# A gated cross-attention and feed-forward block on one core: a load order, a rotary pair and a centring step rewritten

## The chip, the core and the metric

The kernel runs on one NeuronCore of one Trainium2 chip. The core has five engines that run side by side and talk through semaphores: TensorE (PE in the profile: matrix products into PSUM; its weight loads are listed as PEld), VectorE (DVE), ScalarE (ACT), GpSimd (POOL, which reads and writes SBUF only) and SyncE (SP, which here only starts transfers). Each takes its instructions strictly in the order in which the program lists them. The metric is device time in microseconds (us) for the whole program, lower is better.

## What is computed

Four sequences of 1024 tokens with width 256 attend to 154 memory tokens of their own through 4 query heads that share one key and value head, with rotary positions; then comes a feed-forward layer whose weights are rounded to -1, 0 or 1. Both branches are gated by a tanh and added to the residual.

```python
x = x + tanh(g_xattn[0]) * xattn(layernorm(x), ctx_1024, mask)
x = x + tanh(g_ffn[0])   * ffn(layernorm(x))

def xattn(x, mem_seq, mem_mask):
    xn, mn = rmsnorm(x, rms_scale), rmsnorm(mem_seq, rms_scale)   # normed * (1 + scale)
    q = einsum('BTD,NDH->BTNH', xn, q_w)             # 4 heads of 64
    k, v = einsum('BSD,cKDH->cBSKH', mn, kv_w)       # 1 head of 64
    q, k = rope(q, S + arange(T)) * 64 ** -0.5, rope(k, arange(S))
    # rope: [x1 * cos - x2 * sin, x2 * cos + x1 * sin] on the halves of a head
    probs = softmax(where(mem_mask, q @ k, MASK_FILL))
    return einsum('BTNH,NHD->BTD', probs @ v, out_w)

def ffn(x):
    h = gelu(x @ ternary(W1).T + b1)                 # exact gelu, 1024 wide
    return h @ ternary(W2).T + b2
```

## The kernel before, in words

The 4096 tokens are 8 groups (`NG`) of 512 tokens, and a group is 4 tiles (`NT`) of 128 tokens. A group passes three stages: its attention in step i, the first layer of its feed-forward in step i+1 and the second layer in step i+2, so a step of the main loop (`step`) works on three groups at once. Steps 0 and 1 (`FIRST`, `SECOND`), together with what prepares weights, keys and values (`BEFORE`), are the function `fill` of each engine, whose calls are in an order written by hand. Each engine has its own `fill` and its own `step`; nothing else sets the order. Steps 2 to 9 run through `loop`, and their order of calls is the same on either side of the change.

Float32 accuracy is had by splitting an operand into a rounded part and a remainder (`_hi` and `_lo`): ACT copies the rounded part out of PSUM, DVE subtracts it from PSUM and so makes the remainder, and PE multiplies hi by hi, hi by lo and lo by hi. The remainders of the combined value and output weights (`vw_rest`) are made on DVE; the tuple `VW_ON_POOL` that could send some to POOL is empty.

The pieces that the change touches:

- **Queries.** `q(s, t)` and `q_first(s)` project a tile into a PSUM bank `ps_m` (256 columns: head, half, element). `rotate` (L976 to L994) reads the bank twice on DVE: once times the row's norm and the cosines into `q_cos` (L989), once times the norm and the sines into `q_sin` (L992). POOL adds the two with the halves swapped (`add_rotated`, L463), PE transposes the sum (`q_T`, L1447), ACT and DVE split it (`q_hi`, `q_lo`), and PE multiplies it by the keys (`scores`).
- **Centring.** The layer norm's mean is taken out of the query weights instead of the tokens. ACT scales `wq` rows by 1 + `rms_scale` (`scale_wq`, twice 128x256), PE sums them over all 256 inputs with a matrix of ones (`sum_wq`), DVE subtracts the sum divided by 256 (`centre_wq`, L872, twice 128x256), and ACT and DVE split the result into `wq_hi` and `wq_lo`.
- **Loads.** SP starts, in this order: the memory tokens and their four tails, group 0 of x (`x_sb[0]`), the key tables, the query tables, `wo`, `w1t`, `w2t`, group 1 of x (`x_sb[1]`, L349) and `b1`. ACT starts the identity, the scale row, the two gates, `wk`, `wv` and `wq`.
- **Statistics of group 1.** `sums1(FIRST)` (L952, four BN_STATS on DVE) needs group 1 of x.
- **Weights' means.** ACT adds up the absolute values of both weight matrices (`sum_weights`, L638) as soon as each is there; thresholds and ternary weights come from these.

## Time and profile before

| | us |
|---|---|
| median of three runs | 308.63 |
| lowest and highest run | 308.58 and 308.81 |
| the profiled execution: its own time | 309.19 |
| the profiled execution: span of the core | 307.4 |
| PE busy in the span | 295.4 |
| DVE busy | 243.2 |
| ACT busy | 234.3 |
| POOL busy | 131.1 |

The profile records one execution. Its own time is 1.79 us above the span (what lies before the first and after the last instruction) and 0.56 us above the median of the runs. The page gives, for each engine, how long it was busy, and the same in 40 slices with the clock that TensorE was granted. It has a chain of waits followed back from the last instruction, groups of instructions by line, and the transfers. The trace behind it can be asked for the instructions of one engine in order of time, for what an engine waited for, and for busy time by stretches. Matrix products are pipelined, so one listed with 0.28 us may be followed by the next after 0.12 us: what a row of many costs is read from start to start.

### The profile page before, as it was taken

The numbers are of one execution on the slowest core, as the hardware profiler recorded it, in microseconds if no ns is written. First come the engines' busy times: TensorE is split into PE (matmuls) and PEld (weight loads), VectorE is DVE, ScalarE is ACT, GpSimd is POOL, SyncE is SP. The second block draws the span as 40 slices with busy tenths as digits, with TensorE's granted clock in tenths as the row PEclk, the third lists the DMA queues.
The fourth block names the chain that finished last, engine by engine and source line by source line (L and its number), as shares of the span: only waits on it lengthen the run. The fifth ranks groups of instructions, "written<-read, shape, count | busy, mean of one in ns | idle before, by whom it ended". The sixth has DMA issues, their size and how long they took to land.

```text
span 307.4 us, 6780 instructions
## 1 busy us (share of the span) xinstructions
PE 295.4 (96%) x2119; PEld 274.6 (89%) x2119; DVE 243.2 (79%) x819; ACT 234.3 (76%) x601; POOL 131.1 (43%) x152
## 2 busy tenths in 40 slices
PE   5996999989999999999999999999999999999996
PEld 5975999878999899989998899989998999889886
DVE  2589899999987889779886899878977897567443
ACT  2596787898697967897588959796788958883581
POOL 8376878692246305522334414630542333511300
PEclk9999899999999999999999999999999999999999
DMA  6970000200202002100201010100210000100202
GB/s 204 286 243 2 0 3 0 71 0 2 69 3 68 2 0 70 53 17 2 68 13 55 0 54 15 51 17 0 71 52 17 2 0 11 61 3 0 70 0 68
DMA packets 12281, 13.27 MB, mean 43 GB/s; under 512 B 823, under 2 KB 11696, under 8 KB 12256
## 3 DMA queue, kind: packets, MB, share of 16 engines
q1 hardware_dynamic: 11452, 12.29, 12.6%
q10 hardware_dynamic: 708, 0.46, 0.5%
q0 software_dynamic: 96, 0.21, 0.4%
q8 instruction: 13, 0.21, 0.3%
q14 instruction: 12, 0.10, 0.1%
HBM read 8.76 MB, written 4.19 MB: 42 GB/s over the span
## 4 chain that ended last, share of the span: by engine, by line
PE 85%; DVE 7%; issue 2%; ACT 2%; DMA 1%; POOL 0%; ACTq 0%; DVEq 0%
PE ps_m L1293 22%; PE ps_h L1293 22%; PE ps_m L1526 17%; PE ps_s L1293 9%; PE ps_t L1301 4%; PE ps_t L1471 4%; PE ps_t L1447 2%; DMA gate_row<-in_gates 1%; PE ps_t L1546 1%; PE ps_m L1546 1%; DVE s_neg L1025 1%; PE ps_t L1479 1%; DVE pT_lo L938 1%; ACT hT_hi L699 1%; ACT h_all L699 1%
## 5 line engine op out<-in xcount | busy, mean ns | idle before, releaser
L487 POOL TENSOR_TENSOR prob<-prob,p_inv 128x512 f32<-128x512 f32 x32 | 34.2, 1069 | 66.8 <-DVE p_inv L1041 66.7
L1086 DVE TENSOR_TENSOR hT_lo<-h_all,hT_hi 128x512 fp32r<-128x512 f32 x64 | 42.2, 686 | 18.6 <-ACT hT_hi L699 18.6
L1293 PE MATMUL ps_h<-x1nT_hi,w_tern 128*128 128x512 f32 x128 | 54.4, 425 | 1.2 <-ACT hT_hi L699 0.9
L1526 PE MATMUL ps_m<-w_tern,hT_hi 128*128 128x256 f32 x224 | 55.2, 287 | 0.0
L1526 PE MATMUL ps_m<-w_tern,hT_lo 128*128 128x256 f32 x224 | 53.6, 279 | 0.0
L665 ACT ACTIVATE prob<-s_neg,s_min 128x154 f32<-128x154 f32 x128 | 52.4, 416 | 1.2 <-DVE s_min L1036 1.1
L699 ACT ACTIVATE h_all<-ps_h,b_sb 128x512 f32<-128x512 f32 x64 | 44.6, 697 | 8.2 <-PE ps_h L1293 7.0
L1293 PE MATMUL ps_h<-x1nT_lo,w_tern 128*128 128x512 f32 x128 | 50.6, 395 | 0.0
L463 POOL TENSOR_TENSOR q_cos<-q_cos,q_sin 128x256 f32<-128x256 f32 x32 | 23.6, 738 | 58.4 <-DVE q_sin L992 57.6
L1293 PE MATMUL ps_m<-vw_hi,pT_hi 128*128 128x256 f32 (+1 forms) x160 | 45.5, 284 | 0.0
L1293 PE MATMUL ps_m<-vw_hi,pT_lo 128*128 128x256 f32 (+1 forms) x160 | 44.8, 280 | 0.0
L1293 PE MATMUL ps_m<-vw_lo,pT_hi 128*128 128x256 f32 (+1 forms) x160 | 44.7, 279 | 0.0
L699 ACT ACTIVATE hT_hi<-ps_h,b_sb 128x512 fp32r<-128x512 f32 x64 | 44.7, 698 | 0.0
L1526 PEld LDWEIGHTS ps_m<-w_tern,hT_lo 128*128 128x128 f32 x224 | 42.2, 188 | 0.0
L1526 PEld LDWEIGHTS ps_m<-w_tern,hT_hi 128*128 128x128 f32 x224 | 42.1, 188 | 0.0
L938 DVE TENSOR_TENSOR pT_lo<-ps_t,pT_hi 128x512 fp32r<-128x512 f32 (+1 forms) x64 | 30.2, 482 | 10.8 <-ACT pT_hi L642 10.7
L642 ACT ACTIVATE pT_hi<-ps_t 128x512 fp32r<-128x512 f32 (+1 forms) x64 | 27.3, 444 | 9.0 <-PE ps_t L1471 8.8
L1293 PEld LDWEIGHTS ps_m<-vw_hi,pT_hi 128*128 128x128 f32 x160 | 30.0, 188 | 1.2
L1293 PEld LDWEIGHTS ps_h<-x1nT_hi,w_tern 128*128 128x128 f32 x128 | 24.1, 188 | 7.4 <-ACT hT_hi L699 3.8
L1293 PEld LDWEIGHTS ps_m<-vw_lo,pT_hi 128*128 128x128 f32 x160 | 30.1, 188 | 0.6
L1293 PEld LDWEIGHTS ps_m<-vw_hi,pT_lo 128*128 128x128 f32 x160 | 30.0, 187 | 0.0
L642 ACT ACTIVATE qT_hi<-ps_t 128x256 fp32r<-128x256 f32 x32 | 12.1, 377 | 23.2 <-PE ps_t L1447 23.2
(162 smaller groups left out, 778.2 us busy)
## 6 DMA issues: line engine op xcount, KB each, us to landing
x_sb<-in_x SPq DMA_DIRECT2D x8, 512.0 KB, 3.5
out_x<-x_both SPq DMA_DIRECT2D x8, 384.0 KB, 2.5
h_all<-in_w1t SPq DMA_DIRECT2D x1, 1024.0 KB, 11.1
w_raw<-in_w2t SPq DMA_DIRECT2D x1, 1024.0 KB, 13.4
out_x<-x_both SPq DMA_DIRECT2D x8, 128.0 KB, 1.7
x_both<-in_ctx_main SPq DMA_DIRECT2D x1, 512.0 KB
wo_raw<-in_wo SPq DMA_DIRECT2D x2, 256.0 KB, 8.4
...
```

Of the source, the lines that this page charges most:

```text
L463: pool.tensor_tensor(q, q, swapped, ALU.add).then_inc(q_roped, 1)
L487: pool.tensor_tensor(main, main, inv.to_broadcast([P, H, P]), ALU.mult)
L642: nc.scalar.activation(dst, src, ACT.Copy).then_inc(t_hi, 1)
L665: e = nc.scalar.activation(prob[t][:, h, :], s_neg[t % 2][:, h, :], ACT.Exp, bias=s_min[t % 2][:, h:h + 1], scale=-1.0, accum_out=p_sum[:, ...
L699: g = nc.scalar.activation(dst, ps_h[c % 2][:], ACT.Gelu, bias=b1_sb[:, c:c + 1])
L938: dve.tensor_tensor(dst, src, hi, ALU.subtract).then_inc(t_lo, 1)
L1086: dve.tensor_tensor(hT_lo[:, c, :], h_act[c % 4][:], hT_hi[:, c, :], ALU.subtract).then_inc(h_split, 1)
L1293: m = pe.matmul(dst, lhs, rhs, start=(n == 0), stop=(n == len(pairs) - 1))
L1301: m = pe.transpose(dst[:, P * t:P * (t + 1)], src[:, t, P * k:P * (k + 1)], ident_sb[:])
L1447: m = pe.transpose(t_bank(s.i, f"q{t}")[:, P * a:P * (a + 1)], q_cos[t % 2][:, P * a:P * (a + 1)], ident_sb[:])
L1471: m = pe.transpose(t_bank(s.i, f"p{t}")[:, P * h:P * (h + 1)], prob[t][:, h, 0:P], ident_sb[:])
L1526: m = pe.matmul(dst, a[:, c, P * t:P * (t + 1)], w[:, c, :], start=(c == 0 and a is hT_hi), stop=(c == NF - 1 and a is hT_lo))
```

## The change

1. **Second input's load.** SP starts `x_sb[1]` right behind the key tables, ahead of the query tables, `wo` and both weight matrices. Two of the four memory tails move from SP to ACT. On ACT the scale row is now the first transfer and the gates the last, each with a semaphore of its own, so PE spreads the scales without waiting for the gates (`spread_gates` is a step of its own).
2. **Rotary pair.** Cosines and sines lie in one table `rq` [128, 8, 2, 64], and `rotate` is one SCALAR_TENSOR_TENSOR of 512 columns into `q_both`. The query weights' columns are reordered to element, head (`p c h`), so that the table is repeated over the four heads as the innermost direction. POOL's `add_rotated` reads both halves of `q_both` with a step of four elements (16 bytes), back in the order head, half, element, and writes a third buffer `q_sum`. The joined table is built once by POOL from the two loaded ones (`join_tables`: two copies of 128x512), and the first `rotate` waits for that instead of the load.
3. **Centring product.** The centred and scaled weights are one product: a 256x256 matrix `centre` (the identity minus 1/256, each row times 1 + scale), made by POOL, DVE and ACT from 128x128 pieces while loads are under way, times the raw `wq`. PE does four products of 256 columns instead of two, reading `wq` in the new column order (a step of 64 elements, 256 bytes). ACT and DVE split the result straight from PSUM. `scale_wq` on ACT, `sum_wq` on PE and the two DVE operations of `centre_wq` are gone.
4. **Value remainders.** All are on DVE, which the code before did as well: `VW_ON_POOL` is empty on both sides. A like tuple for the gelu's remainders, `SPLIT_ON_POOL`, is new and empty too. Its waits on a pool semaphore stand in the loop's PE code with a count of zero.
5. **Order of `fill`.** All four compute engines have a new order of calls, with the PSUM bank sequence `FILL_T` to match. The order of `step` is unchanged. Group 0's transposed x goes to `x1nT_hi` and `x1nT_lo`, which are free then, so group 1's need not wait for it. Before the first real product PE does nine products of ones on ones instead of five, and the two later fillers (two and four products) are gone.

The core of the diff (new names of semaphores, and the many lines that only move a call, are left out):

```diff
-            for b in range(B):
+            for b in range(2):
                 sp.dma_start(ctx_sb[TP * b:TP * b + TAIL, B, :], ctx_tail[b]).then_inc(ctx_in, 16)
             sp.dma_start(x_sb[0][:], x_g[0]).then_inc(x_in[0], 16)
             sp.dma_start(rk_cos[:], rope_k_cos).then_inc(tab_in, 16)
             sp.dma_start(rk_sin[:], rope_k_sin).then_inc(tab_in, 16)
-            sp.dma_start(rq_cos[:], rope_q_cos).then_inc(rope_in, 16)
-            sp.dma_start(rq_sin[:], rope_q_sin).then_inc(rope_in, 16)
+            sp.dma_start(x_sb[1][:], x_g[1]).then_inc(x_in[1], 16)
+            sp.dma_start(rq_cos, rope_q_cos).then_inc(rope_in, 16)
+            sp.dma_start(rq_sin, rope_q_sin.rearrange("p t j c -> p t (j c)")).then_inc(rope_in, 16)
...
-            sp.dma_start(x_sb[1][:], x_g[1]).then_inc(x_in[1], 16)
...
+            def join_tables():
+                pool.wait_ge(rope_in, 32)
+                pool.tensor_copy(rq[:, :, 0].rearrange("p t (j c) -> p t j c", j=2),
+                                 rq_cos.rearrange("p t (o c) -> p t o c", o=1).to_broadcast(
+                                     [P, 2 * NT, 2, C // 2])).then_inc(rope_set, 1)
+                pool.tensor_copy(rq[:, :, 1], rq_sin).then_inc(rope_set, 1)
...
-                q = q_cos[t % 2][:].rearrange("p (h j c) -> p h j c", h=H, j=2)
-                swapped = q_sin[t % 2][:].rearrange("p (h j c) -> p h j c", h=H, j=2)[:, :, ::-1, :]
-                pool.tensor_tensor(q, q, swapped, ALU.add).then_inc(q_roped, 1)
+                by_head = [q[t % 2].rearrange("p (j c h) -> p h j c", h=H, j=2) for q in (q_cos, q_sin)]
+                pool.tensor_tensor(q_sum[t % 2][:].rearrange("p (h j c) -> p h j c", h=H, j=2), by_head[0],
+                                   by_head[1][:, :, ::-1, :], ALU.add).then_inc(q_roped, 1)
...
-                cos = rq_cos[:, pos, :].rearrange("p (a c) -> p a c", a=1).to_broadcast([P, 2 * H, C // 2])
-                dve.scalar_tensor_tensor(q_cos[t % 2][:].rearrange("p (a c) -> p a c", a=2 * H),
-                                         q.rearrange("p (a c) -> p a c", a=2 * H), r, cos, ALU.mult, ALU.mult)
-                sin = rq_sin[:, pos].rearrange("p (a j) c -> p a (j c)", a=1).to_broadcast([P, H, C])
-                dve.scalar_tensor_tensor(q_sin[t % 2][:].rearrange("p (h c) -> p h c", h=H),
-                                         q.rearrange("p (h c) -> p h c", h=H), r, sin,
+                tables = rq[:, pos].rearrange("p a (c o) -> p a c o", o=1).to_broadcast([P, 2, C, H])
+                twice = q.rearrange("p (o c h) -> p o c h", o=1, h=H).to_broadcast([P, 2, C, H])
+                dve.scalar_tensor_tensor(q_both[t % 2][:].rearrange("p a (c h) -> p a c h", h=H), twice, r, tables,
                                          ALU.mult, ALU.mult).then_inc(m_read, 1)
...
-            def sum_wq():
-                pe.wait_ge(wq_scaled, KD)
-                products(ps_m[0][:, 0:H * C], [(ones_sb[:], wq_s[:, k]) for k in range(KD)]).then_inc(wq_summed, 1)
+            def centre_wq():
+                pe.wait_ge(centre_set, KD)
+                pe.wait_ge(wq_in, 16)
+                for k in range(KD):
+                    m = products(ps_m[0][:, H * C * k:H * C * (k + 1)],
+                                 [(centre[:, j, P * k:P * (k + 1)], wq_raw[:, j].rearrange("p (h c) -> p c h", h=H)) for j in range(KD)])
+                m.then_inc(wq_centred, 1)
...
-            def centre_wq():
-                dve.wait_ge(wq_scaled, KD)
-                dve.wait_ge(wq_summed, 1)
-                for k in range(KD):
-                    dve.scalar_tensor_tensor(wq_s[:, k], ps_m[0][:, 0:H * C], -1.0 / D, wq_s[:, k],
-                                             ALU.mult, ALU.add).then_inc(wq_centred, 1)
```

The new orders, at the three places that matter. **DVE, from the keys' rotation to the first query rotation.** Before (`prob` is the scaled `wq`, the second 128x512 is the rest of group 0's transposed x, `hT_hi` holds the values):

```order
L872 SCALAR_TENSOR_TENSOR prob<-ps_m,prob 128x256 x2
L938 TENSOR_TENSOR xT_lo<-ps_t,xT_hi 128x512
L943 BN_AGGR mv<-bn 128x2 x4
L946 TENSOR_SCALAR ve<-mv 128x4
L877 TENSOR_TENSOR wq_lo<-prob,wq_hi 128x512
L896 TENSOR_SCALAR gate_r<-ctx_r,gate 128x4
L891 TENSOR_TENSOR hT_hi<-ps_m,hT_hi 64x512
L989 SCALAR_TENSOR_TENSOR q_cos<-ps_m,r,rq_cos 128x256
L992 SCALAR_TENSOR_TENSOR q_sin<-ps_m,r,rq_sin 128x256
```

Now:

```order
L940 TENSOR_SCALAR gate_r<-ctx_r,gate 128x4
L996 BN_STATS bn<-x_sb 128x6 x4
L1054 COPY mask_now<-mask_bias 128x154
L982 TENSOR_TENSOR x1nT_lo<-ps_t,x1nT_hi 128x512
L920 TENSOR_TENSOR wq_lo<-ps_m,wq_hi 128x512
L935 TENSOR_TENSOR hT_hi<-ps_m,hT_hi 64x512
L935 TENSOR_TENSOR hT_hi<-ps_h,hT_hi 64x128
L1034 SCALAR_TENSOR_TENSOR q_both<-ps_m,r,rq 128x512
L987 BN_AGGR mv<-bn 128x2 x4
L990 TENSOR_SCALAR ve<-mv 128x4
```

The centring is gone, and group 1's statistics, the mask's copy and the second value remainder have come ahead of the first rotation; before, they stood behind the third. **ACT, from the first weight sum to the first exponentials** (`h_all` and `w_raw` are the two weight matrices, `prob,p_sum` the exponentials of tile 0). Before:

```order
L638 ACTIVATE hT_lo,w_sums<-h_all 128x2048
L642 ACTIVATE qT_hi<-ps_t 128x256
L605 ACTIVATE hT_hi<-ps_h 64x128
L606 ACTIVATE hT_hi<-ps_h 64x128
L642 ACTIVATE xT_hi<-ps_t 128x512
L642 ACTIVATE qT_hi<-ps_t 128x256
L638 ACTIVATE hT_lo,w_sums<-w_raw 128x2048
L642 ACTIVATE xT_hi<-ps_t 128x512
L631 ACTIVATE vw_hi<-ps_h,gate_r 128x512
L665 ACTIVATE prob,p_sum<-s_neg,s_min 128x154 x4
```

Now:

```order
L675 ACTIVATE hT_lo,w_sums<-h_all 128x2048
L679 ACTIVATE qT_hi<-ps_t 128x256 x2
L675 ACTIVATE hT_lo,w_sums<-w_raw 128x2048
L679 ACTIVATE xT_hi<-ps_t 128x512
L668 ACTIVATE vw_hi<-ps_h,gate_r 128x512
L679 ACTIVATE qT_hi<-ps_t 128x256
L702 ACTIVATE prob,p_sum<-s_neg,s_min 128x154 x4
```

The first of group 1's two transposed halves has moved from ahead of the second weight sum to behind it, the second half behind the exponentials, and the small value halves ahead of the first sum. **POOL, from the key tables to the query sums** (`x1n` is the rotated keys, `hT_lo` the remainder of `wo`). Before:

```order
L398 TENSOR_TENSOR rk_sin<-rk_sin,ctx_r 128x320
L404 TENSOR_TENSOR x1n<-s_neg 128x640
L418 TENSOR_TENSOR r<-ve,neghalf 128x4
L408 TENSOR_SCALAR mask_bias<-mask_u 128x616
L463 TENSOR_TENSOR q_cos<-q_cos,q_sin 128x256
L430 TENSOR_TENSOR hT_lo<-wo_raw,hT_lo 128x1024
L463 TENSOR_TENSOR q_cos<-q_cos,q_sin 128x256
```

Now:

```order
L423 TENSOR_TENSOR rk_sin<-rk_sin,ctx_r 128x320
L434 TENSOR_SCALAR mask_bias<-mask_u 128x616
L444 TENSOR_TENSOR r<-ve,neghalf 128x4
L429 TENSOR_TENSOR x1n<-s_neg 128x640
L411 COPY rq<-q_sum 128x8x64
L414 COPY rq<-q_both 128x8x64
L456 TENSOR_TENSOR hT_lo<-wo_raw,hT_lo 128x1024
L488 TENSOR_TENSOR q_sum<-q_both 128x256 x3
```

The two table copies are new ahead of the first query sum, and the remainder of `wo` has moved ahead of it.

## Rows read from the trace of the kernel before

**Rows 1.** Chain of waits, first scores of steps 2 and 7: start, length.

```profile
81.44 1.10 PE ps_s L1293 x6
...
249.55 0.92 PE ps_s L1293 x6
```

**Rows 2.** Busy time by stretch: length, PE, PEld, DVE, ACT, POOL, clock, DMA, GB/s.

```profile
24.00:29.50 5.50, 3.47 (x24) 2.83 (x24) 5.41 (x25) 3.56 (x6) 3.14 (x7) 1.00 0.00 0
29.50:34.50 5.00, 5.00 (x26) 4.83 (x27) 4.09 (x21) 3.46 (x13) 4.53 (x5) 0.66 0.00 2
34.50:60.00 25.50, 25.09 (x195) 23.77 (x195) 24.93 (x95) 21.36 (x75) 19.54 (x21) 1.00 0.07 22
79.30:280.00 200.70, 199.57 (x1472) 187.28 (x1471) 164.14 (x560) 161.89 (x424) 74.33 (x88) 1.00 0.09 30
```

**Rows 3.** ACT in order of time: start, length, line, operation [idle before, releaser].

```profile
15.80 1.06 ACT L618 ACTIVATE hT_lo<-wo_raw 128x1024 fp32r<-128x1024 f32 x1
...
17.72 0.59 ACT L605 ACTIVATE hT_hi<-ps_m 64x512 fp32r<-64x512 f32 x1 [0.23 <-PE ps_m L1293]
...
19.15 1.50 ACT L614 ACTIVATE kk_hi<-ps_s 64x512 fp32r<-64x512 f32 x4 [0.23 <-PE ps_s L1374]
20.67 1.91 ACT L638 ACTIVATE hT_lo<-h_all 128x2048 fp32r<-128x2048 f32 x1
...
22.70 0.38 ACT L642 ACTIVATE qT_hi<-ps_t 128x256 fp32r<-128x256 f32 x1
22.98 0.26 ACT L605 ACTIVATE hT_hi<-ps_h 64x128 fp32r<-64x128 f32 x1
...
26.27 1.90 ACT L638 ACTIVATE hT_lo<-w_raw 128x2048 fp32r<-128x2048 f32 x1
...
29.30 0.69 ACT L631 ACTIVATE vw_hi<-ps_h,gate_r 128x512 fp32r<-128x512 f32 x1 [0.56 <-PE ps_h L1293]
29.89 0.42 ACT L665 ACTIVATE prob<-s_neg,s_min 128x154 f32<-128x154 f32 x1
```

**Rows 4.** PE in order of time, before 18 us (the keys' products are L1293 x20).

```profile
10.88 1.06 PE L1301 MATMUL ps_t<-ident_sb,x_sb 128*128 128x128 f32 x4
11.73 2.92 PE L1293 MATMUL ps_h<-x1n,prob 128*128 128x64 f32 x20
14.49 0.61 PE L1301 MATMUL ps_t<-ident_sb,x_sb 128*128 128x128 f32 x4
14.93 1.03 PE L1293 MATMUL ps_m<-prob,ones_sb 128*128 128x256 f32 x4
```

**Rows 5.** Transfers: issue to landing of both loads of x; GB/s in 40 slices.

```profile
DMA to landing us min/median/max: 7.3/10.7/14.2
...
GB/s 204 286 243 2 0 3 0 71 0 2 69 3 68 2 0 70 53 17 2 68 13 55 0 54 15 51 17 0 71 52 17 2 0 11 61 3 0 70 0 68
```

**Rows 6.** DVE in order of time: a rotary pair, statistics, a 512-column form.

```profile
22.55 0.48 DVE L989 SCALAR_TENSOR_TENSOR q_cos<-ps_m,r,rq_cos 128x256 f32<-128x256 f32 x1
22.95 0.47 DVE L992 SCALAR_TENSOR_TENSOR q_sin<-ps_m,r,rq_sin 128x256 f32<-128x256 f32 x1
...
24.46 1.39 DVE L952 BATCH_NORM_STATS2 bn<-x_sb 128x6 f32<-128x256 f32 x4
...
46.83 0.74 DVE L916 SCALAR_TENSOR_TENSOR vw_lo<-ps_h,gate_r,vw_hi 128x512 fp32r<-128x512 f32 x1
```

**Rows 7.** POOL in order of time: query sums (L463), remainder of `wo`, costliest 256 columns.

```profile
20.93 0.74 POOL L463 TENSOR_TENSOR q_cos<-q_cos,q_sin 128x256 f32<-128x256 f32 x1 [0.84 <-DVE q_sin L992]
21.63 2.36 POOL L430 TENSOR_TENSOR hT_lo<-wo_raw,hT_lo 128x1024 fp32r<-128x1024 f32 x1
...
44.20 0.93 POOL L414 TENSOR_SCALAR b_gated<-x_both,gate 128x256 f32<-128x256 f32 x1
...
183.13 1.52 POOL L463 TENSOR_TENSOR q_cos<-q_cos,q_sin 128x256 f32<-128x256 f32 x2 [6.58 <-DVE q_sin L992]
```

**Rows 8.** PE in order of time: the transpose that waits for the first sum of step 5.

```profile
184.00 0.38 PE L1447 MATMUL ps_t<-ident_sb,q_cos 128*128 128x128 f32 x2
```

428 lines of the change are left out of this document (236 added, 192 removed), and 8 rows, old and new, of the table FILL_T.

## The prediction

> **What bounds the kernel now.** I read the busy time by stretches first. In the loop [rows 2] PE is busy 199.57 of 200.70 us, DVE 164.14 and ACT 161.89. The chain of waits agrees: the first scores of step 2 begin at 81.44 and those of step 7 at 249.55 [rows 1], five steps in 168.11 us, 33.6 us each, and nearly every piece between is PE's. What the loop's DVE saves is therefore worth nothing there; only what delays PE counts. The fill is another stage. From 24.0 to 29.5 us PE is busy 3.47 of 5.50 us and DVE 5.41 [rows 2]: PE waits for DVE. From 29.5 to 34.5 PE is busy throughout, but at a granted clock of 0.66, which loses 0.34 x 5 = 1.7 us of full-speed work; what went before was the 2.0 us of idling. From 34.5 to 60 PE has 25.09 and DVE 24.93 of 25.50 us: both are full. So the question is how much earlier the fill gets to its first exponentials (29.89, [rows 3]), and whether the loop keeps its 33.6 us.
>
> **The chain I cost: ACT in the fill.** Between the copy of `wo` and the first exponentials ACT is the engine with the fewest choices, since it must sum both weight matrices there. Before it takes 29.89 - 15.80 = 14.1 us, with idle stretches in it, the last of 0.56 us [rows 3]. In the new order, from the start of the copy of `wo`: that copy 1.06, two halves of the values 2 x 0.59 = 1.18, the two small halves 2 x 0.26 = 0.52, keys 1.50, first weight sum 22.70 - 20.67 = 2.03, two query halves at 22.98 - 22.70 = 0.28 each 0.56, second weight sum 1.90, one transposed half and one `vw_hi` at 29.89 - 29.30 = 0.59 each 1.18, a third query half 0.28. Sum 10.2 us [rows 3]. It holds if nobody makes ACT wait, and the copy of `wo` begins when `wq_hi` is done and `wo` is there.
>
> When is that? PE must have transposed group 0's x and made the keys' products and the centring product. The loads begin as before; group 0's x lands 7.3 us after its start [rows 5], and PE takes it at 10.88 behind a filler [rows 4]. I put its landing at 10.5. Two of the tails are no longer ahead of it on SP, a few tenths that I leave uncounted. From start to start four transposes take 11.73 - 10.88 = 0.85 and the keys' products 14.49 - 11.73 = 2.76; the next four transposes take 14.93 - 14.49 = 0.44 [rows 4]. So PE's pace doubled about 14.5 us, from its lower level (1.2 GHz) to its upper one (2.4 GHz), and the first two of these figures would halve at the upper. The centring product is new. Two products of 256 columns are listed with 1.03; four transposes listed with 0.61 cost 0.44, so the tail is 0.17 and four products cost 2 x 0.86 = 1.72 at the upper level, 3.44 at the lower.
> Pace doubling when it did: 10.5 + 0.85 + 0.85 + 2.76 + 1.72 = 16.7, and 0.6 for ACT's copy makes 17.3. Upper level throughout: 10.5 + 0.44 + 0.44 + 1.38 + 1.72 + 0.6 = 15.1. Lower throughout: 10.5 + 1.7 + 2.76 + 3.44 + 0.6 = 19.0. The nine fillers at the start are denser than five were, but a pause until x lands follows; I take 17.3. `wo` allows it: ACT took it at 15.80 without waiting [rows 3], and 0.52 MB of x in front, at 243 to 286 GB/s [rows 5], puts it back by 1.8 to 2.2 us, to 18.0 at the very latest.
> First exponentials: 17.3 + 10.2 = 27.5, a gain of **2.4 us** (15.1: 4.6; 19.0: 0.7).
>
> A page speaks against the centring product. No row has a product whose moving operand is read with a step; the Trainium skill, "SBUF — State Buffer", section "Door 1: The DMA port swizzle", says that SBUF has lines of 16 bytes and that every access to a new line costs extra; here each column of `wq` is 256 bytes from the last. The page gives no price. Were the product to take twice as long, 1.7 us of the 2.4 would go.
>
> **The other parts.** Centring leaves DVE (two operations of 256 columns) and ACT; both stood before 18 us, and the product's time above already pays for it. The statistics of group 1, 1.39 us on DVE at 24.46 [rows 6], move into the time when DVE waits for the keys' products and `wq_hi`. They need x to have landed; its load is started behind the key tables instead of at the end, and by the bytes ahead it comes some 2 us behind group 0's. This removes PE's wait in the 24.0 to 29.5 stretch, so ACT's sum above is not held up by it. It is part of the 2.4, not an addition.
>
> **Rotary pair.** Two forms of 256 columns: 22.95 - 22.55 = 0.40 and about as much again, 0.79 in all. A 256-column form is listed with 0.47, a 512-column one with 0.74 [rows 6], so 256 columns more cost 0.27, and the joined form takes 0.40 + 0.27 = 0.67. That saves 0.12 per tile. Bound from the other side: if reading the table with a step of zero costs, no row shows it; at 0.79 nothing is saved. Of the fill's nine rotations the five behind the first exponentials lie in the stretch where DVE is full: 5 x 0.12 = **0.6 us**. The four before it are inside the first term. In the loop: nothing, PE sets the pace.
>
> **Joined table.** Two copies of 512 columns on POOL, priced by the costliest 256 columns there, 0.93 [rows 7], at 1.9 each at most, and by the cheapest, a sum of 0.74 without its start, at about 1.2. That is 2.4 to 3.8 us, then the remainder of `wo`, 2.36, and the first sum, 0.74. What hides them is ACT's first weight sum: ACT asks for the first query half only at 17.3 + 1.06 + 1.18 + 0.52 + 1.50 + 2.03 = 23.6. Keys rotated at about 16.5 to 17, POOL is done at 22.0 to 23.9. The cover just holds; where it fails it costs 0.3. I count 0.
>
> **POOL's sum in the loop.** It now reads both inputs with a step of 16 bytes. In step 5 two sums take 1.52, so the first is done at 183.13 + 0.76 = 183.89, and PE transposes it at 184.00 [rows 7, 8]: 0.11 us of room, and the other steps look alike. DVE's 0.12 makes it 0.23. Rows of POOL reading with a step there are none. By the nearest, 0.74 and 0.93 for 256 columns [rows 7], the sum grows by 0 to 0.19 and stays inside the room: **0**. PE's extra wait on a count of zero, and the empty value part, cost 0 too: the first is one more instruction in a queue that runs ahead, the second changes nothing.
>
> **Sum.** 2.4 + 0.6 = 3.0. The profiled execution would go from 309.19 to 306.2, its span from 307.4 to 304.4. The median of the runs lies 0.56 below: 308.63 - 3.0 = **305.6 us**.
>
> **Rivals.**
> (a) *No slow stretch.* The 1.7 us at clock 0.66 come after PE idled. If the fuller order leaves no such gap, they are gained as well: 303.9. For it: the idle 2.0 us are what the new order removes. Against: PE still waits between 18 and 24 us for the first queries, and a new gap there may bring the same lower level.
> (b) *POOL's step costs half as much again.* A sum of 1.11 is 0.37 longer; less the room of 0.23 PE loses 0.14 in each of six steps, 0.8, and the first sum of the fill 0.4 on its path: 305.6 + 1.2 = 306.8. The Trainium skill, "GPSIMD Engine Reference", section "Performance pitfalls for Q7 kernels", states this: reading with steps above 8 bytes costs about 50% more per element. No row here shows it.
> (c) *Slower: the same sum becomes PE's bound.* The gain of 3.0 over six steps is 0.5 each; with the room of 0.23, a sum longer by 0.73, so from 1.47 us on (twice today's), eats it all. At 1.85 (two and a half times) PE loses 0.88 x 6 = 5.3: 310.9. Against it: the dearest comparable row is 0.93.
> (d) *The head start is given back.* `wo` and both weight matrices land some 2 us later. PE now stands at the total of the weights (`total_weights`) between the first and the second scores, and cannot go on until ACT's second sum is done. If that sum begins at its old 26.27, the exponentials come at 26.27 + 1.90 + 1.18 + 0.28 = 29.6, 0.3 earlier than before. With the 0.6 of the rotations the gain is 0.9: 307.7.
>
> **How the numbers follow.** My case has 0.45, (a) 0.15, (b) 0.18, (c) 0.10, (d) 0.12. A measurement of this kernel tells about 0.2% (0.6 us) from no change, so faster means below 308.0. Faster: 0.45 + 0.15 + 0.18 and a quarter of (d), 0.81. Same: most of the rest of (d), 0.08. Slower: (c) and 0.01 of (d), 0.11. My case by itself runs from 303.4 (exponentials 4.6 us earlier) to 307.3 (0.7). The range takes in (a) with some more head start and (b) with less of it: 302.6 to 308.0; outside are (c), the far ends of (a) and some of (d).
>
> **What would show it.** Right: first exponentials at about 27.5; the form of 512 columns listed with 0.74; steps of 33.6 us; the first scores of step 2 near 78.4. Wrong if the centring product takes over 2 us, if POOL's sum is listed above 0.97 us and the steps grow, if a slow stretch is longer than before, or if ACT idles ahead of a weight sum.

## The result, and the profile after

The changed kernel is slower, by 1.9%. Its median is 314.69 us (four runs, 313.97 to 315.12) beside 308.61 us for the kernel before in the same comparison: a ratio of 1.0194 with a 95% interval of 1.0173 to 1.0214. The forecast was 305.6 us with a range of 302.6 to 308.0, so the miss is 9.1 us, and the sign is wrong. The profiled execution took 314.87 us, its span is 313.1 us.

The same stretches as in [rows 2], of the kernel after (length, PE, PEld, DVE, ACT, POOL, clock, DMA, GB/s):

```profile
24.00:29.50 5.50, 4.26 (x26) 3.11 (x26) 5.37 (x16) 4.49 (x10) 2.67 (x3) 1.00 0.00 1
29.50:34.50 5.00, 4.53 (x32) 4.00 (x33) 4.97 (x17) 5.00 (x15) 4.45 (x8) 1.00 0.01 2
34.50:60.00 25.50, 24.10 (x185) 22.71 (x184) 25.33 (x97) 20.16 (x73) 24.95 (x25) 1.00 0.01 3
79.30:280.00 200.70, 199.03 (x1457) 185.66 (x1456) 165.82 (x536) 160.09 (x420) 85.29 (x89) 1.00 0.09 30
```

The slow stretch at clock 0.66 is gone, as rival (a) had it, and the time is longer all the same. The new thing is the third line: POOL is busy 24.95 of 25.50 us, where it was at 19.54 [rows 2]. In the same stretch of `a_pool_unit` (below), where the sum is as short as before, it is busy 24.05, so most of this rise comes with the new order, and the longer sums take what was left. In the loop POOL rose from 74.33 to 85.29, and PE lost half a microsecond of work.

PE at the start, in order of time, as in [rows 4]:

```profile
7.01 1.95 PE L1379 MATMUL ps_s<-ident_sb,x_both 128*128 128x128 f32 x8
...
10.09 0.58 PE L1372 MATMUL ps_m<-gate_row,ones_sb 1*128 1x2 f32 x2 [0.69 <-DMA gate_row<-in_gates]
10.60 1.97 PE L1345 MATMUL ps_t<-ident_sb,x_sb 128*128 128x128 f32 x8
12.37 4.37 PE L1337 MATMUL ps_h<-x1n,prob 128*128 128x64 f32 x20
16.52 3.81 PE L1337 MATMUL ps_m<-x_both,prob 128*128 128x256 f32 x8
20.16 2.02 PE L1337 MATMUL ps_m<-prob 128*128 128x512 f32 x4
```

Read from start to start: eight transposes of x take 1.77, the keys' products 4.15 (2.76 before, [rows 4]), the centring product 3.64, where the forecast had 1.72. ACT in order of time, as in [rows 3]: the copy of `wo`, both weight sums and the first exponentials.

```profile
20.86 1.05 ACT L655 ACTIVATE hT_lo<-wo_raw 128x1024 fp32r<-128x1024 f32 x1
...
25.56 1.91 ACT L675 ACTIVATE hT_lo<-h_all 128x2048 fp32r<-128x2048 f32 x1
...
29.16 1.91 ACT L675 ACTIVATE hT_lo<-w_raw 128x2048 fp32r<-128x2048 f32 x1
...
32.37 0.44 ACT L702 ACTIVATE prob<-s_neg,s_min 128x154 f32<-128x154 f32 x1
```

The first exponentials come at 32.37, 2.5 us later than before and 4.9 later than forecast. The two operations of the rotary path, as groups (count, busy us, mean ns), and the first scores of steps 2 and 7 on PE, which answer to [rows 1] (in this view step 7 of the kernel before begins at 249.39):

```profile
L488 POOL TENSOR_TENSOR q_sum<-q_both 128x256 f32<-128x256 f32 x32 | 37.1, 1168 | 58.8 <-DVE q_both L1034 58.8
...
L1034 DVE SCALAR_TENSOR_TENSOR q_both<-ps_m,r,rq 128x512 f32<-128x512 f32 x32 | 23.5, 744 | 1.4 <-PE ps_m L1337 1.4
```

```profile
84.94 0.40 PE L1337 MATMUL ps_s<-kk_hi,qT_hi 128*128 x1 [0.36 <-DVE qT_lo L982]
...
254.64 0.37 PE L1337 MATMUL ps_s<-kk_hi,qT_hi 128*128 128x308 f32 x1
```

The joined operation is listed with 0.744 us, as forecast. POOL's sum takes 1.168 us where it took 0.74 [rows 7]. A step takes (254.64 - 84.94) / 5 = 33.94 us instead of 33.6. So of the 5.7 us by which the span grew, 3.5 are there at the first scores of step 2 (84.94 against 81.44), 1.7 come in the five steps to step 7 (254.64 against 249.39), and 0.5 behind.

### The profile page after: what moved, and what is told of

It reads as the page before. It is cut to its first block, busy times and chain, and to the rows that moved or that the text cites. A ratio compares the mean times of both kernels' runs of the same rounds, so it can differ in the third digit from the quotient of the medians.

```text
span 313.1 us, 6764 instructions
## 1 busy us (share of the span) xinstructions
PE 301.6 (96%) x2119; PEld 277.0 (88%) x2119; DVE 246.6 (79%) x786; ACT 234.0 (75%) x601; POOL 145.6 (46%) x155
## 4 chain that ended last, share of the span: by engine, by line
PE 38%; issue 26%; DVE 16%; POOL 14%; DMA 2%; ACT 2%; ACTq 1%; POOLq 0%; DVEq 0%
PE ps_h L1337 10%; PE ps_m L1580 10%; PE ps_m L1337 8%; POOL q_sum L488 5%; POOL prob L521 4%; PE ps_s L1337 2%; POOL r L444 2%; DVE s_neg L1066 2%; DVE vw_lo L960 2%; DVE q_both L1034 2%; PE ps_t L1345 2%; DMA gate_row<-in_gates 2%; PE ps_t L1525 2%; DVE w_tern L977 1%; POOL x_both L506 1%
## 5 line engine op out<-in xcount | busy, mean ns | idle before, releaser
L521 POOL TENSOR_TENSOR prob<-prob,p_inv 128x512 f32<-128x512 f32 x32 | 34.7, 1084 | 65.8 <-DVE p_inv L1082 65.8
L488 POOL TENSOR_TENSOR q_sum<-q_both 128x256 f32<-128x256 f32 x32 | 37.1, 1168 | 58.8 <-DVE q_both L1034 58.8
## 6 DMA issues: line engine op xcount, KB each, us to landing
wo_raw<-in_wo SPq DMA_DIRECT2D x2, 256.0 KB, 10.2
```

The lines of the kernel that those rows point to most:

```text
L488: pool.tensor_tensor(q_sum[t % 2][:].rearrange("p (h j c) -> p h j c", h=H, j=2), by_head[0], by_head[1][:, :, ::-1, :], ALU.add).then_inc ...
L521: pool.tensor_tensor(main, main, inv.to_broadcast([P, H, P]), ALU.mult)
```

## Experiments

Each kernel is told by its edit against the changed kernel or the one before. Each group of runs shared its runs of the kernel before on one chip, whose medians were 308.62, 308.92, 308.42 and 309.1 us. In the profiles of the changed kernel and its variants PE takes group 0 of x between 8.34 and 11.35 us, as its load lands, and the runs of one kernel lie 1 to 4 us apart; I give the range. Where two profiles are compared, the time at which x was taken has to be subtracted first.

### POOL's step

`a_pool_unit`: the changed kernel, with POOL's inputs read in memory order.

```diff
-                by_head = [q[t % 2].rearrange("p (j c h) -> p h j c", h=H, j=2) for q in (q_cos, q_sin)]
+                by_head = [q[t % 2].rearrange("p (h j c) -> p h j c", h=H, j=2) for q in (q_cos, q_sin)]
```

> The changed kernel with one edit: POOL's sum reads both inputs in order instead of with a step of 16 bytes (so the query columns come out permuted and the output is not the reference's; every instruction keeps its size). Theory: the step in POOL's reads is what lengthens the loop. The sum goes from 1.17 to 0.74 us, steps from 33.95 back to 33.6 or less, six of them give 2 us and the fill 0.5 to 1: about 312.0 instead of 314.7. Rival: the loop grows by something else (the added wait of PE, the joined operation); the sum falls to 0.74 and the steps stay at 33.95, 314 to 314.7.

Measured: 308.18 us (306.17 to 310.31, ten runs), ratio to the kernel before 0.9977 (0.9932 to 1.0022). The sum takes 0.735 us; the first scores of steps 2 and 7 begin at 78.82 and 246.67, 33.57 us a step. The mechanism is the expected one. The gain of 6.5 us in the medians is over twice what I had expected, but part of it is TensorE's level, the subject of the next section. The runs fall into two groups: five with a median of 307.12 (mean clock 1.00 in each; the profiled one is among them and has its keys' products at the upper level, 2.18 us) and five with a median of 309.46 (mean clock 0.983 in four). Group beside group, 309.46 against 314.69 of the changed kernel, and 307.12 against the 312.2 that it takes with fillers (below), the step in POOL's reads costs 5.1 to 5.2 us.

`b_pool_step`: the kernel before, with the same step put into its sum (into the write too, since this sum is made in place).

```diff
-                q = q_cos[t % 2][:].rearrange("p (h j c) -> p h j c", h=H, j=2)
-                swapped = q_sin[t % 2][:].rearrange("p (h j c) -> p h j c", h=H, j=2)[:, :, ::-1, :]
+                q = q_cos[t % 2][:].rearrange("p (j c h) -> p h j c", h=H, j=2)
+                swapped = q_sin[t % 2][:].rearrange("p (j c h) -> p h j c", h=H, j=2)[:, :, ::-1, :]
```

> The kernel before with one edit: POOL's sum reads and writes with a step of 16 bytes (output permuted, not the reference's). Theory: the sum takes 1.17 us there too, and beyond the 0.11 us of room PE loses 0.32 in each of six steps, 1.9, and about 0.5 in the fill: 308.6 becomes 311.0. Rival: the fill and loop of before hide it, under 309.2.

Measured: 310.84 us (310.42 to 311.78), ratio 1.0079 (1.0063 to 1.0096). Its steps take (250.50 - 80.54) / 5 = 33.99 us, 0.4 more than before. Put into the old order of `fill`, the step costs 2.2 us, about 2 of it in the loop; put into the new order, it costs more. What differs is POOL's load in `fill`. In the changed kernel POOL works from 36 to 60 us without a gap. From its timeline:

```profile
42.65 1.18 POOL L488 TENSOR_TENSOR q_sum<-q_both 128x256 f32<-128x256 f32 x1
43.78 1.49 POOL L521 TENSOR_TENSOR prob<-prob,p_inv 128x512 f32<-128x512 f32 x1
45.24 0.36 POOL L522 TENSOR_TENSOR prob_tail<-prob,p_inv 128x104 f32<-128x104 f32 x1
45.56 1.18 POOL L488 TENSOR_TENSOR q_sum<-q_both 128x256 f32<-128x256 f32 x1
46.73 1.55 POOL L482 TENSOR_SCALAR hT_lo<-h_all,w_thr 128x512 fp32r<-128x512 f32 x1
```

No row has an idle time behind it: the scaled exponentials (L521), which PE transposes next, stand in the queue behind the longer sums. What this costs PE is seen in `a_unit_wq_gates` (below), which has the step in POOL's reads and is otherwise `a_all_unit_joined`. Between the first exponentials and 59 us its PE waits three times:

```profile
31.16 0.38 PE L1337 MATMUL ps_s<-kk_hi,qT_hi 128*128 128x308 f32 x1 [0.76 <-DVE s_min L1066]
47.12 0.63 PE L1525 MATMUL ps_t<-ident_sb,prob 128*128 128x128 f32 x4 [0.44 <-DVE pT_lo L982]
55.47 0.66 PE L1525 MATMUL ps_t<-ident_sb,prob 128*128 128x128 f32 x4 [0.25 <-POOL prob_tail L522]
```

Without the step none of the three is there, and the stretch to the first scores of step 2 is 1.4 us shorter. Two of the waits name DVE, so the step reaches PE mostly through others, and how is not traced further.

### TensorE's level at the start, and the step in the centring product

The keys' products at 4.15 us and the centring product at 3.64 had two possible causes: TensorE at 1.2 instead of 2.4 GHz, or, for the second, the 256 bytes between the columns of `wq`.

`a_unit_wq`: the changed kernel, `wq` read in memory order.

```diff
-                                 [(centre[:, j, P * k:P * (k + 1)], wq_raw[:, j].rearrange("p (h c) -> p c h", h=H)) for j in range(KD)])
+                                 [(centre[:, j, P * k:P * (k + 1)], wq_raw[:, j]) for j in range(KD)])
```

> The changed kernel with one edit: the centring product reads wq in memory order instead of with a step of 256 bytes (weights permuted, output not the reference's). Theory A, the stride: the four products fall from 3.64 to about 1.8 us and the time by 1 to 1.8. Theory B, TensorE's lower level (1.2 GHz): they stay at 3.6, the time within 0.3 of 314.7.

Measured: 313.79 us (310.67 to 314.86, four runs), ratio 1.0104 (0.9979 to 1.023). The product takes 19.39 - 15.88 = 3.51 us, against 3.64 with the step. PE of this kernel:

```profile
11.71 4.37 PE L1337 MATMUL ps_h<-x1n,prob 128*128 128x64 f32 x20
15.88 3.73 PE L1337 MATMUL ps_m<-x_both,prob 128*128 128x256 f32 x8
19.39 2.54 PE L1337 MATMUL ps_m<-prob 128*128 128x512 f32 x4
```

That looked like theory B, and it would have been wrong to stop there: the keys' products at 4.17 us say that this was measured at the lower level.

`a_gates_late`: the changed kernel, the gates spread behind group 0's transposes, with fillers in the gap.

```diff
-                spread_gates()
+                keep_warm(3)
                 x_T(BEFORE, 0)
                 x_T(BEFORE, 1)
+                spread_gates()
...
-                gates_tanh()
                 x_hi(BEFORE, 0)
...
                 x_hi(BEFORE, 1)
+                gates_tanh()
```

> The changed kernel with the spread of the gates moved from ahead of group 0's transposes to behind them on PE (and the tanh behind both rounded copies on ACT), with three filler products where PE stood idle for the gates. Theory: the idle 0.69 us at 9.4 keeps PE at its lower level until 20; without it the pace doubles near 14 as in the kernel before, the centring takes 1.8, the copy of wo starts near 18 instead of 20.9, and the time falls by 1.5 to 3. Rival: the level rises no earlier, 0.0 to 0.5 gained.

Measured: 312.18 us (310.88 to 312.66, ten runs), ratio 1.009 (1.0051 to 1.0128). No run is near 314 any more. That is 2.5 us below the first set of the changed kernel and 1.4 below the second (`a_again`, below). PE:

```profile
12.46 3.71 PE L1337 MATMUL ps_m<-x_both,prob 128*128 128x256 f32 x8
16.00 1.90 PE L1337 MATMUL ps_m<-prob 128*128 128x512 f32 x4
```

TensorE was at its upper level (keys' products 2.28 us), and the product took 3.54 us all the same, not the expected 1.8. The last experiment takes the step out here.

`a_unit_wq_gates`: `a_gates_late` with the edit of `a_unit_wq`.

> a_gates_late with the centring product reading wq in memory order (weights permuted, output not the reference's); POOL keeps its step. At TensorE's upper level the four products took 3.54 us with the step. If the step is what doubles them, they take 1.75 here and the time falls from 312.2 by 1 to 1.8. If something else bounds them, they stay at 3.5 and the time at 312.2. At the lower level both forms take 3.5 to 3.6.

Measured: 310.91 us (310.43 to 312.0, ten runs), ratio 1.0078 (1.0051 to 1.0104). PE and the copy of `wo` on ACT:

```profile
12.57 1.95 PE L1337 MATMUL ps_m<-x_both,prob 128*128 128x256 f32 x8
14.35 1.88 PE L1337 MATMUL ps_m<-prob 128*128 128x512 f32 x4
```

```profile
16.67 1.06 ACT L655 ACTIVATE hT_lo<-wo_raw 128x1024 fp32r<-128x1024 f32 x1 [1.52 <-DMA wo_raw<-in_wo]
```

So the product takes 1.78 us in order and 3.54 with the step at 2.4 GHz, 3.51 and 3.64 at 1.2 GHz. The step doubles it at the upper level and is nearly hidden at the lower one. The Trainium skill, "SBUF — State Buffer", section "Door 1: The DMA port swizzle", on which the forecast drew, says that an access to a new line of 16 bytes costs extra. The trace agrees: with a step of 256 bytes there is an extra cost, and it is a factor of two here. Of the 1.76 us less, the copy of `wo` shows 0.8 (17.47 to 16.67): ACT now waits 1.52 us for the load of `wo`, 0.66 in `a_gates_late`.

`a_again`: the changed kernel itself once more.

> The changed kernel itself, unchanged, beside the others, to see how its executions spread. If the level at which TensorE runs between 5 and 20 us differs from one execution to the next, there are two groups about 3 us apart, near 311 and 314.5; if the gates' wait settles it always, all are at 314 to 315.

Measured: 313.54 us (311.42, 312.48, 314.60, 315.39), two groups about 3 us apart. PE's level in the profiled one of them (314.60 us), by stretches, same columns as above:

```profile
7.00:8.50 1.50, 1.40 (x10) 1.28 (x10) 1.50 (x5) 1.34 (x3) 0.11 (x1) 1.00 1.13 368
8.50:10.00 1.50, 0.30 (x3) 0.26 (x2) 1.40 (x10) 1.20 (x4) 0.31 (x1) 0.66 1.02 331
10.00:12.00 2.00, 2.00 (x10) 1.98 (x11) 0.91 (x3) 0.77 (x3) 1.86 (x3) 0.50 1.03 258
12.00:16.00 4.00, 4.00 (x22) 4.00 (x20) 1.29 (x7) 1.08 (x5) 1.88 (x3) 0.50 1.02 262
```

Between 8.5 and 10.0 PE is busy 0.30 of 1.50 us, since it stands 1.20 us for the gates, and the granted clock falls from 1.00 to 0.50 there, the lower of its two levels. It stays at 0.50 until past 19 us although PE is busy throughout. In the first profile of the changed kernel the column says 1.00 all the time, and the pace is half until 20 us: 0.22 us a transpose, where 0.12 is the upper level's. A level that TensorE already had at the start isn't in that column; the pace of the transposes tells it.

`a_fill_gap`: the changed kernel with three fillers in the gap, nothing moved.

```diff
+                keep_warm(3)
                 spread_gates()
                 x_T(BEFORE, 0)
```

> The changed kernel with one edit: three filler products on PE where it stood idle for the gates; nothing is moved. Theory: TensorE's fall to the lower level (or its staying there) comes from the idle stretch at 9 us; without it no run is in the group of 314 to 315, all are at 311 to 312.7. Rival: the late placing of the gates did it in a_gates_late, and here runs at 314 to 315 remain.

Measured: 312.23 us (312.04 to 313.23, four runs), ratio 1.0128 (1.0107 to 1.0148). The group at 314 to 315 is gone, as in `a_gates_late`: the three products do it, wherever the gates stand (one run of the four is above the expected 312.7). In its profile the clock is at 0.54 from 9 to 11 us, PE having stood 1.43 us for a memory tail, and is back at 1.00 by 12.8.

`b_no_filler`: the kernel before without its two fillers ahead of group 0's transposes.

```diff
                 context_T(1)
-                keep_warm(2)
                 x_T(BEFORE, 0)
```

> The kernel before with one edit: the two filler products ahead of group 0's transposes are left out, so PE idles up to 0.9 us until x has landed. Theory: in some or all runs TensorE now stays at or falls to its lower level, the keys' products take 4.1 us and not 2.2 to 2.8, and these runs are 1.5 to 3 slower: median 309.5 to 311.5. Rival: an idle stretch this short does nothing, within 0.3 of the kernel before.

Measured: 311.59 us (310.38 to 312.35, four runs), ratio 1.0096 (1.0069 to 1.0123). Two products that compute nothing are worth about 3 us of the kernel before. PE without them:

```profile
9.98 1.06 PE L1301 MATMUL ps_t<-ident_sb,x_sb 128*128 128x128 f32 x4
11.06 4.50 PE L1293 MATMUL ps_h<-x1n,prob 128*128 128x64 f32 x20
15.35 1.06 PE L1301 MATMUL ps_t<-ident_sb,x_sb 128*128 128x128 f32 x4
```

The keys' products take 4.29 us, and the level rises only behind 18 us. The expected mechanism is only half seen: PE idles 0.2 us here, not 0.9, since x had landed.

So the fillers are shown to help. That they do it by closing an idle time is not. In the profile of `a_pool_unit` PE stands 1.01 us for the gates, and neither the clock (1.00) nor the pace falls:

```profile
9.27 0.38 PE L1372 MATMUL ps_m<-gate_row,ones_sb 1*128 1x2 f32 x2 [1.01 <-DMA gate_row<-in_gates]
9.57 1.09 PE L1345 MATMUL ps_t<-ident_sb,x_sb 128*128 128x128 f32 x8
```

In `a_unit_wq` PE waits for neither the gates nor x and keeps the slow pace all the same. Both there and in the first profile of the changed kernel the pace is already 0.22 us a transpose at 7 us, ahead of the gates, so in these two the wait for the gates isn't where the level was lost. In `c_write` (below) it is as slow at 7 us; there three fillers follow, and at 10.4 us the transposes run at nearly the upper level:

```profile
6.93 1.98 PE L1381 MATMUL ps_s<-ident_sb,x_both 128*128 128x128 f32 x8
...
10.40 1.18 PE L1347 MATMUL ps_t<-ident_sb,x_sb 128*128 128x128 f32 x8
```

### What the forecast's gain was, with the three things taken out

`a_all_unit_joined`: the edits of `a_pool_unit`, `a_unit_wq` and `a_gates_late` together.

> The same as a_all_unit_pair, but the rotary pair is one operation of 512 columns (columns permuted, so the output is not the reference's). Theory: the joined form saves 0.12 us per rotation where DVE is full, five times in the fill, 0.6 in all: 0.3 to 0.8 faster than a_all_unit_pair. Rival: no difference.

`a_all_unit_pair`: the same, but two rotary operations of 256 columns.

```diff
-                dve.scalar_tensor_tensor(q_both[t % 2][:].rearrange("p a (c h) -> p a c h", h=H), twice, r, tables,
-                                         ALU.mult, ALU.mult).then_inc(m_read, 1)
+                for a, dst in enumerate((q_cos, q_sin)):
+                    table = rq[:, pos, a].rearrange("p (o c) -> p o c", o=1).to_broadcast([P, H, C])
+                    m = dve.scalar_tensor_tensor(dst[t % 2].rearrange("p (h c) -> p h c", h=H),
+                                                 q.rearrange("p (h c) -> p h c", h=H), r, table, ALU.mult, ALU.mult)
```

> The changed kernel with every operand read in memory order: the rotary pair as two operations of 256 columns again, query columns in the old order, POOL's sum and the centring product without a step, and the gates spread behind group 0's transposes as in a_gates_late. It computes everything. Theory: the forecast's gain was there and three things took it (POOL's step, the product's step of 256 bytes, TensorE's late rise). Then the sum takes 0.74 us, the four centring products 1.8 with TensorE at its upper level, steps 33.6, and the time is 304.5 to 306. Rival: the new order of the fill is itself worse, 308 or more.

Measured: joined 305.93 us (305.18 to 306.45, four runs), ratio 0.99 (0.9841 to 0.9958); pair 308.39 us (307.14 to 310.13, ten runs), ratio 0.9974 (0.9939 to 1.001). A second set of twelve runs of the pair (`a_pair_again`, below) gave 307.39. The pair misses its expected 304.5 to 306; the first set is in the range of the rival, that the new order of `fill` is itself worse, and both sets are only 0.25% (0.8 us) below the kernel before. The joined form, expected 0.3 to 0.8 faster than the pair, is 2.5 us faster in the medians.

Joined against `a_unit_wq_gates`, which differs from it in POOL's step alone, gives the price of that step in the new order: 310.91 - 305.93 = 5.0 us in the medians. In the two profiles (spans 308.6 and 303.4) 0.7 of 5.2 is that x came earlier (transposes at 9.01 and 8.34); 0.7 lies between there and the first exponentials, 1.4 from these to the first scores of step 2 (52.58 and 51.19 us), 1.9 in five steps (33.95 and 33.57 each), 0.5 behind.

Pair against joined from the first exponentials to the first scores of step 2: 51.68 and 51.19 us, 0.5 saved by the joined form, and 0.07 in each step. Another 0.25 lies between the copy of `wo` and the first exponentials (10.84 and 10.59). That is 1.1 us of the 2.5 by which the spans differ (305.9 and 303.4); another 1.1 is that x was taken at 9.44 and 8.34. Why the medians lie 2.5 us apart stays open.

### A complete kernel with the joined form

The kernels of this section and `c_write_wo` also have the centring product in memory order and the gates late, with fillers, as in `a_unit_wq_gates`.

`c_full`: joined form, POOL adds in the columns' own order, PE transposes every second column, the keys' rows interleaved to match, and ACT and DVE write the split of the query weights with a step of 16 bytes. Its core:

```diff
+                pool.tensor_tensor(q_sum[t % 2][:].rearrange("p (j n) -> p j n", j=2), cos,
+                                   sin[:, ::-1, :], ALU.add).then_inc(q_roped, 1)
...
-                                     q_sum[t % 2][:, P * a:P * (a + 1)],
+                                     q_sum[t % 2][:, a::2],
...
+                nc.scalar.activation(wq_hi[:].rearrange("p k (c h) -> p k h c", h=H),
+                                     ps_m[0][:].rearrange("p (k h c) -> p k h c", k=KD, h=H), ACT.Copy).then_inc(wq_hi_set, 1)
```

> A complete kernel with the joined rotary operation and no long step in any read: the query columns stay in the order element, head; POOL adds in memory order; PE transposes every second column (heads a and a+2 of the four, a step of 8 bytes); the keys' rows are interleaved to match, with a parity factor in the keys' split; the centring product reads wq in memory order and its split writes the new column order; gates spread late. Theory: it behaves like a_all_unit_joined, 305.2 to 306.5, with the sum at 0.74 us and the centring product at 1.8; 2 to 3 us below the kernel before. Rival: the step of 8 bytes in PE's load, or the strided writes of the split, cost what was saved: a transpose pair above 0.44 us from start to start or a copy above 0.7, and 307.5 or more.

> The kernel of a_all_unit_pair again, beside c_full on the same chip, to price the joined rotary operation. Forecast's price: 0.12 us per rotation, nine in the fill, two or three of them off the path: 0.6 to 1.1 slower than c_full. Its medians until now were 2.4 apart from the joined form's, four runs against ten. If that difference is real, 307.5 to 308.5 here.

Measured: `c_full` 307.68 us (307.38 to 308.99, twelve runs), ratio 0.9975 (0.9954 to 0.9996); `a_pair_again` 307.39 us (306.46 to 309.76), ratio 0.9975 (0.9956 to 0.9993). `c_full` misses its 305.2 to 306.5, and the rival holds: what the joined form saves is given back. Groups of `c_full`:

```profile
L1508 PEld LDWEIGHTS ps_t<-ident_sb,q_sum 128*128 128x128 f32 x64 | 10.4, 205 | 0.1
...
L926 DVE TENSOR_TENSOR wq_lo<-ps_m,wq_hi 128x512 fp32r<-128x512 f32 x1 | 1.1, 1133 | 0.0
L639 ACT ACTIVATE wq_hi<-ps_m 128x512 fp32r<-128x512 f32 x1 | 1.1, 1132 | 3.2 <-PE ps_m L1345 3.2
```

PE's load of q with a step of 8 bytes takes 0.205 us, 0.141 in the changed kernel, and its steps are 33.78 us long instead of 33.57. The split's two operations take 1.13 us each; reading and writing in order, in `a_pair_again`, they take 0.60 and 0.67.

`c_write`: the joined form, and POOL's step moved from its two reads to its one write. The split reads PSUM with the step instead of writing SBUF with it.

```diff
-                by_head = [q[t % 2].rearrange("p (j c h) -> p h j c", h=H, j=2) for q in (q_cos, q_sin)]
-                pool.tensor_tensor(q_sum[t % 2][:].rearrange("p (h j c) -> p h j c", h=H, j=2), by_head[0],
-                                   by_head[1][:, :, ::-1, :], ALU.add).then_inc(q_roped, 1)
+                cos, sin = (q[t % 2].rearrange("p (j c h) -> p j c h", h=H, j=2) for q in (q_cos, q_sin))
+                pool.tensor_tensor(q_sum[t % 2][:].rearrange("p (h j c) -> p j c h", h=H, j=2), cos,
+                                   sin[:, ::-1], ALU.add).then_inc(q_roped, 1)
```

> A complete kernel: the joined rotary operation stays, and POOL's sum walks in the order of the joined columns, so both reads are in memory order and only its one write has a step (64 elements, 256 bytes) back to head order; PE and keys are as in the changed kernel. The centring product reads wq in memory order, and its split reads PSUM with the step and writes in order. Gates spread late. Theory: a step costs POOL in its reads alone; the sum takes 0.74 us, steps 33.6, time 305.5 to 307. Rival A: a step in the write costs the same, sum 1.17, steps 34.0, 310 to 311. Rival B: the sum lies between, 0.9, and the time near 308.

Measured: 306.66 us (305.85 to 307.12, six runs), ratio 0.9926 (0.9903 to 0.9948), 33.58 us a step, as expected. By the ratios it is 1.5 us below the pair. Its groups:

```profile
L488 POOL TENSOR_TENSOR q_sum<-q_both 128x256 f32<-128x256 f32 x32 | 23.7, 746 | 61.5 <-DVE q_both L1036 61.3
...
L922 DVE TENSOR_TENSOR wq_lo<-ps_m,wq_hi 128x512 fp32r<-128x512 f32 x1 | 0.7, 676 | 0.0
L637 ACT ACTIVATE wq_hi<-ps_m 128x512 fp32r<-128x512 f32 x1 | 0.6, 598 | 3.2 <-PE ps_m L1339 3.2
```

The same sum with the same three tensors takes 0.746 us: the step costs POOL in its reads alone. Source and destination may be walked in either order, and the change walked in the order of the destination.

### The load order

`c_write_wo`: `c_write`, with `wo` loaded ahead of group 1 of x and the query tables.

```diff
             sp.dma_start(rk_sin[:], rope_k_sin).then_inc(tab_in, 16)
+            for r in (0, C):
+                sp.dma_start(wo_raw[r:r + C], wo).then_inc(wo_in, 16)
             sp.dma_start(x_sb[1][:], x_g[1]).then_inc(x_in[1], 16)
```

> c_write with the load of wo started ahead of group 1 of x and the query tables. In a_all_unit_pair, a_unit_wq_gates and c_full the copy of wo stood 0.9 to 2.1 us for its load. Theory: that wait is what the new load order costs; it falls below 0.5 and the time by 0.5 to 1.2 against c_write. Rival: group 1 of x lands later, DVE waits for its statistics ahead of the split of group 0, and nothing or less than nothing is gained.

Measured: 305.31 us (304.66 to 306.20, six runs), ratio 0.9893 (0.9869 to 0.9917): the fastest complete kernel, 1.35 us below `c_write` in the medians (1.2 in the means, known to 0.7) and clearly below the kernel before. On ACT the copy of `wo` and the first exponentials, on PE the first scores of steps 2 and 7:

```profile
14.93 1.05 ACT L656 ACTIVATE hT_lo<-wo_raw 128x1024 fp32r<-128x1024 f32 x1
...
26.22 0.43 ACT L703 ACTIVATE prob<-s_neg,s_min 128x154 f32<-128x154 f32 x1
```

```profile
77.35 0.41 PE L1339 MATMUL ps_s<-kk_hi,qT_hi 128*128 x1 [0.36 <-DVE qT_lo L984]
...
245.20 0.38 PE L1339 MATMUL ps_s<-kk_hi,qT_hi 128*128 128x308 f32 x1
```

ACT no longer waits for `wo` (0.73 us in `c_write`). DVE waits 0.71 us for group 1 of x instead, as the rival had it: the remainder of the query weights comes late, PE waits 0.29 us for it, and ACT later 0.78 us for the first transposed queries, 0.36 in `c_write`. In this pair of profiles little is left of the gain at the first exponentials: they are at 26.22 and 28.02, but x was taken at 8.90 and 10.40, and from the centring product to the exponentials it is 13.77 and 13.91 us. So the gain is shown by the medians, and the way to it isn't. One that would fit: the earlier x lands, the longer the chain ahead of the copy would stand for `wo`.

`b_x1_early`: the kernel before with the early load of group 1 alone.

> The kernel before with the first part of the change alone: group 1 of x is loaded behind the key tables. Nothing else is moved, so group 1's statistics still stand behind the third rotation and had their data already. Theory: no gain, and wo and the weights land 1 to 2 us later: 308.4 to 309.5. Rival: ACT stands for wo and the weight sums, 309.5 or more.

Measured: 309.83 us (308.64 to 312.59, ten runs), ratio 1.0042 (1.0017 to 1.0066). The early load by itself costs 0.5 to 2 us by the interval. In the profile (308.64 us, the fastest of the ten) ACT waits for `wo`:

```profile
17.00 1.06 ACT L618 ACTIVATE hT_lo<-wo_raw 128x1024 fp32r<-128x1024 f32 x1 [2.28 <-DMA wo_raw<-in_wo]
```

## Why the prediction was wrong

**What bounds the kernel now** was read rightly: the first exponentials and the loop's step are the two points through which the result can be followed, and DVE's savings in the loop are worth next to nothing (0.07 us a step).

**POOL's sum, counted at 0, is the largest miss, about 5 us.** Three things failed in that step. The duration was bounded by rows that read in order (growth of 0 to 0.19 us), and it grew by 0.43: rival (b) had the right mechanism and almost the size (1.11 us against 1.168; the rule of the Trainium skill, "GPSIMD Engine Reference", section "Performance pitfalls for Q7 kernels", is +50%, and the traces show +58%). The room was over-read: the sum of step 5 ended 0.11 us ahead of PE's transpose, but in the after trace PE starts 0.08 us behind the sum's end even when it waits for nothing else, so 0.03 was room. The same place now:

```profile
187.57 2.29 POOL L488 TENSOR_TENSOR q_sum<-q_both 128x256 f32<-128x256 f32 x2 [6.12 <-DVE q_both L1034]
```

```profile
188.43 0.28 PE L1337 MATMUL ps_m<-wq_hi,xT_lo 128*128 128x256 f32 x1
188.80 0.44 PE L1500 MATMUL ps_t<-ident_sb,q_sum 128*128 128x128 f32 x2
```

The first of the two sums ends at about 188.72, half of the listed 2.29 behind its start, and PE, free at 188.55 (products follow each other by 0.12 here), starts at 188.80. That is 0.25 us a step; the other 0.1 must lie at another wait, which I have not traced. And rival (b) priced the loop (0.8) and the first sum of the fill (0.4), but not POOL's queue from 36 to 60 us. [rows 2] showed POOL at 19.54 of 25.50 there; the new order by itself brought it to 24.05 (`a_pool_unit`), and four sums longer by 0.43 left no gap. The waits of PE that go with it are worth 1.4 us.

**The start of the copy of `wo`, 17.3 in the sum, was 20.86.** By its terms, forecast and measured: x taken 10.5 and 10.60; eight transposes 1.70 and 1.77; keys' products 2.76 and 4.15; centring product 1.72 and 3.64; ACT's copy 0.6 and 0.70. Two terms carry all of it. The keys' 2.76 was no price of either level: TensorE rose in the middle of it in the kernel before; at the lower level it is 4.15 to 4.29, at the upper 2.2 to 2.3. The end "upper level throughout" halved a mixed figure to 1.38, where 2.2 is right. My end "lower throughout", 19.0, was itself mixed; worked out rightly it is 10.5 + 1.7 + 4.15 + 3.5 + 0.6 = 20.45, within 0.4 of what came. The centring product is 3.5 at either level, for two different reasons, and the sentence "Were the product to take twice as long, 1.7 us of the 2.4 would go" was the truth at the upper level. The forecast saw that the pause until x lands might matter, but its sum took the level of before as given.

**From that copy to the first exponentials**, 10.2 forecast, it took 11.5; with the sum at 0.74 it took 10.6 in three profiles (10.59 in `a_all_unit_joined`, 10.57 in `c_full`, 10.60 in `c_write`), 10.86 in `a_pool_unit` and 11.29 in `c_write_wo`. The rest of 0.4 is ACT waiting for the first transposed queries (0.36 us in `c_write`, 0.78 in the changed kernel). ACT's first weight sum was to hide POOL, a cover that just held in the forecast and didn't in the trace; it wasn't the joined table that broke it, since that was done at 20.54 and POOL then waited for DVE's first rotation (0.86 us ahead of the sum at 25.22).

**The rotary pair** is right in the price of the operation, 0.744 us listed, and near in the stretch that was priced: 0.5 us saved between the exponentials and step 2 where 0.6 was forecast. What it is worth to the whole kernel was put too low: 1.1 us in the traces, 1.5 to 2.5 in the medians. **The joined table** was cheaper than feared, 0.62 and 0.61 us.

**Rival (c)**, slower by POOL's sum, needed 1.47 us to eat up a gain of 3.0. At 1.168 the sum already cost 5.0, since the rival priced only the loop. **Rival (d)**, the head start given back, was looked for at the second weight sum. It sat at the copy of `wo` instead: the forecast had written that `wo` allows its 17.3 and lands at "18.0 at the very latest". As soon as the chain ahead of it was fast, that landing was the bound (16.67 in `a_unit_wq_gates`), and it came as late as 18.19 in `c_full` and 18.91 in `a_pair_again`. It is worth 1.35 us between the medians of `c_write` and `c_write_wo`.

In sum: POOL's step 5.0, TensorE's lower level about 2 (313.5 to 314.7 against 312.2), the step in the centring product about 1.3, the landing of `wo` 1.35. Together 9.7 beside a miss of 9.1; they overlap, and the medians they come from are known to some half a microsecond, the last two worse. With all four taken out the kernel stands at 305.31 us, where the forecast had put it, and its omissions were larger than its gain. That the two figures agree is in part luck: the load order of this kernel isn't the one that was forecast, and the parts came out otherwise, with x taken at 8.90 instead of 10.5 in its profile, the joined form worth more than 0.6 and the rest worth less than 2.4, since the pair, with the new order and no step, is only 0.8 us below the kernel before (it still waits for `wo`).

What stays open: which run of work on PE lifts its level, why `b_no_filler` stayed low with an idle time of 0.2 us only and `a_unit_wq` with none at the gates, while `a_pool_unit` kept the upper level over 1.01 us. The runs show that two or three fillers decide it, not by what rule. Open too are the other 0.1 us of a step and the worth of the joined form.
